# Graph network of eight convolutions on one core: edge rows stay in their PSUM bank through product and scans, TensorE mixes the two Eve scans and adds the residual, swish becomes one activation

## The chip, the cores and the metric

One Trainium2 chip, one of its cores. The metric is the device time of one execution in microseconds (us); lower is better. The kernel before takes 11591.99 us, the median of 3 runs (11556.57 to 11599.9).

## The reference

Node rows `x` (100000 x 128, float32) go through eight graph convolutions, one after the other. There are 50000 edges `src -> dst`, sorted by `dst`. Everything is float32.

```python
# three GCN layers
norm = dinv[src2] * ew2 * dinv[dst2]
out = segment_sum(norm[:, None] * (x @ W)[src2], dst2) + b     # then a residual, batch norm and relu
# two Eve layers
p = relu(x @ wpool.T + bpool); m = p[src]
xmax, xmin = segment_max(m, dst), segment_min(m, dst)           # 0 for a node without edges
eve = relu(wconv[0] * xmax + wconv[1] * xmin + bconv[0])
out = x @ wself.T + eve @ weve.T + bias                         # relu after the first; layer norm of (out + x0) after the second
# two Sage layers
out = segment_mean(x[src], dst) @ W_l.T + b + x @ W_r.T         # h * sigmoid(h) after the first; layer norm of (out + x0) after the second
# one attention layer (GAT) at the end, not touched here
```

## The kernel before, in words

The program runs in stages, with a barrier after each: constants, index tables, degrees (`deg`), the GCN stages `m0`, `m1`, `m2`, a stage `n3` of nodes alone, the Eve stages `m4` (ends with relu) and `m5` (ends with a layer norm, adds the residual stream `x0`), the Sage stages `m6` (ends with swish) and `m7` (ends with a layer norm, adds `x0`), and the attention stage `g8`. The tiles of `m0` to `m7` all have the prefix `m_` in the profile, those of `g8` have `g_`.

A stage `m0` to `m7` does two things at once. **Edges** come in 49 chunks of 1024 (`CH`), a chunk in two halves of 512. GpSimd (POOL) gathers a chunk's rows by 8 indirect DMAs of 128 rows (L1011), and it later scatters the chunk's results into the table `sums` by 8 more (L1019); in between it copies 16 indices for a chunk (L998). In its program the scatters of a chunk come four or five chunks after the gathers. TensorE turns a half with four transposes into a PSUM bank (`e_turn`, `turn_half`, L1060). VectorE (DVE) then reduces over runs of edges with the same `dst` with `tensor_tensor_scan` along the free axis, with a 0/1 mask `same_run`. TensorE multiplies the result with the weights (`multiply_half`, L1070, bank `e_out`), and VectorE writes it to `result`, from where it is scattered. **Nodes** come in 49 pairs of chunks (a unit). SP loads `y`, `x0` where there is one, and `sums` (`load_nodes`, L1095 to L1104) into one buffer for each chunk of a pair, then issues a fill of the next stage's `sums` (L1111). TensorE turns `y` (L1128), ScalarE (ACT) copies it to `nodeT` (L1154, L1156), TensorE multiplies (L1139), VectorE adds `sums`, ScalarE finishes and issues the store.

`merged_sweep` sets the order on every engine but POOL: an edge unit of two chunks (four halves), then the node units whose sums are ready, at most two for an edge unit. Each engine runs its part in program order. SP issues a unit's load of `sums` after it has waited for the scatters that it depends on (L1103).

What the change touches, by stage:

- **GCN edges** (`m0` to `m2`): in `m1` and `m2` ScalarE copies the bank with a scale and a shift to the SBUF tile `hT` (L1293). `weigh` (L1308) multiplies with the weights `w_all` into `hT`, from `hT` in `m1` and `m2`, from the bank in `m0`. The scan (L1329) reads `hT`.
- **GCN nodes**: `res_b = residual + sums`, both in SBUF, 128x1024 elements for one chunk (L1615).
- **Eve edges** (`m4`, `m5`): ScalarE copies the bank to `xT` (L1419), TensorE multiplies by `wpool` (L1375, bank `pool`), ScalarE takes relu to the SBUF tile `pT` (L1433). VectorE scans `hi` (max, L1462) and `lo` (min, L1467) from `pT`, then mixes: `mix = lo * wconv[1] + bconv` (L1474) and `mix = hi * wconv[0] + mix` (L1478). ScalarE takes relu of `mix` (L1407), TensorE multiplies.
- **Norm nodes** (`m5`, `m7`): `part = sums + x0`, both in SBUF, 128x1024 for one chunk (L1717), then `z` = bank + `part` (L1732). The layer norm is applied by ScalarE in sixteen activations for a unit (L743).
- **Swish nodes** (`m6`): ScalarE takes the sigmoid of `z` into `o` (L1774), VectorE multiplies `o * z`, both in SBUF, 128x1024 for one chunk (L1752).

The scan of the Sage stages (L1529) reads its edge rows from the PSUM bank `e_turn` already.

## Time and profile before

| | |
|---|---|
| Median of 3 runs | 11591.99 us (11556.57 to 11599.9) |
| Profiled execution: span from its first to its last instruction | 11581.2 us |
| Median less the span of the profiled execution | 10.8 us |
| PE busy | 6121.9 us (53%) |
| DVE busy | 6779.3 us (59%) |
| ACT busy | 4593.8 us (40%) |
| POOL busy | 7662.4 us (66%) |
| Mean granted TensorE clock | 0.752 of full speed |

The page gives no other time of the profiled execution than its span. Busy shares are means over stages that differ: the seven convolution stages take some 7,750 us of the span, `g8` some 2,250, `n3` some 560. An engine's busy time counts neither its DMA issues (for SP and ACT) nor its waits. On POOL an indirect DMA does count, for the time in which POOL makes its descriptors.

### The profile page before, as it was taken

Reading aid. Unit: us, or ns where it says so; the run is one execution under the profiler, and the core shown is the slowest. Engines: PE = TensorE matmul, PEld = TensorE weight load, DVE = VectorE, ACT = ScalarE, POOL = GpSimd, SP = SyncE. Lnnn points to the kernel's source line nnn. Section 1 sums busy time; section 2 is a strip of 40 time slices with the busy share of each in tenths; the row PEclk is TensorE's granted clock in tenths of the full one; section 3 lists DMA queues with packets and bytes.
Section 4 is the critical chain, followed back from the end, with each engine's and each line's share of the span. In section 5 each row is a group of like instructions: output and inputs, shape, how many; then the busy total and the mean of one; then the engine's idle time right before and its main releaser. Section 6 shows DMA issues by size and latency. Waiting matters only on the chain. (4 is left out here: it accounts for less than half of the span.)

```text
span 11581.2 us, 165045 instructions
## 1 busy us (share of the span) xinstructions
PE 6121.9 (53%) x35574; PEld 4955.3 (43%) x35575; DVE 6779.3 (59%) x16578; ACT 4593.8 (40%) x8654; POOL 7662.4 (66%) x7581
## 2 busy tenths in 40 slices
PE   1005666666566669865655554554454544444443
PEld 1005565566565653354444443544454422222221
DVE  3325555555555556555547775444466647777777
ACT  1111211222222225444435554333355546666665
POOL 4657776777677750177777775777777765666652
PEclk6557887788788889887877777777677766676675
DMA  5997777888788878676657776766688833333322
GB/s 140 223 192 230 260 253 232 283 296 302 250 290 301 297 260 285 224 244 239 226 199 270 259 256 201 256 240 241 216 313 285 291 107 106 110 102 111 110 96 79
DMA packets 1864913, 2570.41 MB, mean 222 GB/s; under 512 B 255773, under 2 KB 1369141, under 8 KB 1864662
## 3 DMA queue, kind: packets, MB, share of 16 engines
q1 hardware_dynamic: 1134168, 1627.27, 42.3%
q10 hardware_dynamic: 504726, 564.87, 14.9%
q0 software_dynamic: 225792, 375.94, 10.1%
q14 instruction: 169, 1.38, 0.0%
q8 instruction: 58, 0.95, 0.0%
HBM read 1499.62 MB, written 1129.98 MB: 227 GB/s over the span
## 5 line engine op out<-in xcount | busy, mean ns | idle before, releaser
L1128 PE MATMUL m_n_bank<-k_ident,m_in_y 128*128 128x128 f32 x5488 | 1009.4, 355 | 1549.2 <-DMA m_in_y<-node_rows_a 396.1
L1019 POOL DMA_INDIRECT sums_gcn<-m_result,m_idx x1176 | 1305.4, 1110 | 420.7 <-issue 348.6
L1128 PEld LDWEIGHTS m_n_bank<-k_ident,m_in_y 128*128 128x128 f32 x5488 | 865.9, 186 | 1648.7 <-issue 1067.6
L1011 POOL DMA_INDIRECT m_rows<-node_rows_a,m_idx x1176 | 1217.6, 1035 | 339.4 <-issue 335.2
L1154 ACT ACTIVATE m_nodeT<-m_n_bank 128x512 f32<-128x512 f32 x980 | 547.3, 597 | 1985.9 <-PE m_n_bank L1128 1973.0
L1019 POOL DMA_INDIRECT sums_eve<-m_result,m_idx x784 | 857.1, 1093 | 348.1 <-issue 231.9
L1019 POOL DMA_INDIRECT sums_sage<-m_result,m_idx x784 | 800.9, 1022 | 263.2 <-issue 230.7
L1011 POOL DMA_INDIRECT m_rows<-node_rows_b,m_idx x784 | 798.2, 1018 | 226.2 <-issue 225.2
L1060 PE MATMUL m_e_turn<-k_ident,m_rows 128*128 128x128 f32 x2744 | 529.5, 328 | 691.1 <-DVE m_sums L1529 327.0
L2181 POOL DMA_INDIRECT sums_gat<-g_result,g_idx x392 | 427.2, 1090 | 669.6 <-DVE g_result L2437 555.8
L1628 DVE SCALAR_TENSOR_TENSOR m_acc<-m_n_bank,m_scales,m_res_b 128x128 f32<-128x128 f32 (+1 forms) x2352 | 634.1, 342 | 264.7 <-PE m_n_bank L1139 204.3
L1060 PEld LDWEIGHTS m_e_turn<-k_ident,m_rows 128*128 128x128 f32 x2744 | 415.3, 173 | 816.4 <-DVE m_sums L1529 319.9
L1573 PE MATMUL m_gram<-m_y 128*128 128x129 f32 (+1 forms) x4800 | 613.1, 288 | 151.2 <-ACT m_y L1599 149.6
L743 ACT ACTIVATE m_o<-m_z,m_ln_shift,m_ln_scale 128x128 f32<-128x128 f32 x1600 | 626.4, 479 | 163.4 <-DMA node_rows_c<-m_o 105.4
L1905 POOL DMA_INDIRECT degree<-deg_deg_slot,deg_place_slot x392 | 452.0, 1153 | 327.4 <-DVE deg_deg_slot L1982 216.9
L1573 PEld LDWEIGHTS m_gram<-m_y 128*128 128x128 f32 (+1 forms) x4800 | 585.1, 201 | 174.8 <-ACT m_y L1599 173.4
L1615 DVE TENSOR_TENSOR m_res_b<-m_in_x,m_in_sums 128x1024 f32<-128x1024 f32 x196 | 240.2, 1226 | 648.0 <-DMA m_in_sums<-sums_gcn 646.5
L1156 ACT ACTIVATE m_nodeT<-m_n_bank,k_bn 128x512 f32<-128x512 f32 x392 | 285.5, 776 | 826.3 <-PE m_n_bank L1128 825.8
L1139 PE MATMUL m_n_bank<-k_gcn,m_nodeT 128*128 128x128 f32 (+1 forms) x4704 | 606.3, 285 | 0.0
L1070 PE MATMUL m_e_out<-k_gcn,m_sums 128*128 128x128 f32 x2352 | 417.3, 333 | 322.8 <-DVE m_result L1341 322.0
L1139 PEld LDWEIGHTS m_n_bank<-k_gcn,m_nodeT 128*128 128x128 f32 (+1 forms) x4704 | 586.8, 203 | 0.0
L998 POOL COPY m_idx<-k_edge_idx 128x16 int32 (+1 forms) x350 | 107.7, 310 | 715.9 <-POOLq L104 715.1
(295 smaller groups left out, 17377.3 us busy)
## 6 DMA issues: line engine op xcount, KB each, us to landing
m_in_sums<-sums_gcn SPq DMA_DIRECT2D x291, 512.0 KB
m_in_y<-node_rows_a SPq DMA_DIRECT2D x291, 512.0 KB
sums_gcn<-k_gcn_b SPq DMA_DIRECT2D x194, 512.0 KB
node_rows_a<-m_y ACTq DMA_DIRECT2D x194, 512.0 KB
...
```

What stands on the lines that cost most here:

```text
L743: ins = act.activation(out[0:n, j, :], z[0:n, j, :], ACT.Identity, bias=self.shift[copy][0:n, at:at + 1], scale=self.scale[copy][0:n, at:a ...
L1011: pool.indirect_dma_start(self.rows[b][:, t, :], None, self.table[:, :], bass.IndirectOffsetOnAxis(self.idx[s][:, t:t + 1], 0)).then_inc(s ...
L1019: pool.indirect_dma_start(self.node_sums[:, :], bass.IndirectOffsetOnAxis(self.idx[s][:, T + t:T + t + 1], 0), self.result[b][:, t, :], No ...
L1060: mm = pe.transpose(bank[:, n * P:(n + 1) * P], self.rows[b][:, H * (i % 2) + n, 0:D], self.k["ident"][:, :])
L1070: mm = pe.matmul(bank[:, n * D:(n + 1) * D], lhs[:, n * P:(n + 1) * P], weight[:, :], start=True, stop=True)
L1128: mm = pe.transpose(self.n_bank[i][:, t * P:t * P + n], self.buf["y"][i // 2][0:n, H * (i % 2) + t, :], self.k["ident"][0:n, 0:n])
L1139: mm = pe.matmul(self.n_bank[i][0:n, t * D:(t + 1) * D], self.nodeT[:, i, t * P:t * P + n], weight[:, :], start=True, stop=True)
L1154: act.activation(out, src, ACT.Copy).then_inc(self.n_turn_read, 1)
L1573: mm = pe.matmul(self.gram[:, 0:D + 1], self.y1[b][0:rows[b], t, 0:D], self.y1[b][0:rows[b], t, :], start=False, stop=False, skip_group_ch ...
L1628: ins = dve.scalar_tensor_tensor(out=self.acc[b][0:n, tt, :], in0=ph.node_out(i, n)[:, t, :], scalar=self.scales[b][0:n, tt:tt + 1], in1=s ...
L1905: pool.indirect_dma_start(self.dram["degree"][:, :], bass.IndirectOffsetOnAxis(self.place_slot[s][:, t:t + 1], 0), self.deg_slot[b][:, t:t ...
L2181: pool.indirect_dma_start(self.node_sums[:, :], bass.IndirectOffsetOnAxis(self.idx[s][:, T + t:T + t + 1], 0), self.result[b][:, t, :], No ...
```

## The change

The copies `hT`, `pT` and `part` in SBUF go. Products and relus write back into the PSUM bank that they read, and the scans read the bank. So a bank is free for the next half only after the scan (GCN: `self.summed`; Eve: the bank holds the pooled rows, then the mix, until `mix_relu`). In Eve, TensorE makes the mix with two 128x512 matmuls with diagonal matrices `mix_w` (made once, among the constants), and ScalarE adds the bias in its relu. The order of TensorE's and ScalarE's steps within an Eve edge unit changes. In the norm stages TensorE adds `x0` in the bank with an identity matmul of 128x512 ahead of each bank's product. `res_b` is made in four pieces of 256 elements. Swish is one `Silu` activation.

```diff
+PIECE = 2
 # constants, VectorE, once
+                for i in (1, 2):
+                    for m in range(2):
+                        dve.tensor_scalar(k[f"mix{i}"][:, m, :], k["ident"][:, :], k[f"wconv{i}"][:, m:m + 1], None, ALU.mult).then_inc(mix_made, 1)
...
 # Conv.multiply_nodes
+            if add:
+                if i % 2 == 0:
+                    self.have(pe, add, m, i // 2)
+                half = self.buf[add][i // 2][0:n, H * (i % 2):H * (i % 2) + H, :]
+                mm = pe.matmul(self.n_bank[i][0:n, :], self.k["ident"][0:n, 0:n], half.rearrange("p t f -> p (t f)"), start=True, stop=False)
+                if i % 2:
+                    mm.then_inc(self.used[add], 1)
             for t in range(H):
                 mm = pe.matmul(self.n_bank[i][0:n, t * D:(t + 1) * D], self.nodeT[:, i, t * P:t * P + n], weight[:, :],
-                               start=True, stop=True)
+                               start=not add, stop=not add or t == H - 1)
...
 # GcnEdges
-                self.ph.turn_half(pe, j, par, q, i, self.turn_free)
+                self.ph.turn_half(pe, j, par, q, i, self.summed)
...
-            act.activation(self.hT[:, i % 2, :], ph.e_turn[i % ph.turn_banks][:, :], ACT.Identity, bias=ss[:, 1:2],
-                           scale=ss[:, 0:1]).then_inc(ph.e_turn_read, 1)
+            act.activation(bank[:, :], bank[:, :], ACT.Identity, bias=ss[:, 1:2], scale=ss[:, 0:1]).then_inc(ph.e_turn_read, 1)
...
-        dve.tensor_tensor(self.hT[:, i % 2, :], src, w, ALU.mult).then_inc(self.weighted, 1)
+        dve.tensor_tensor(bank[:, :], bank[:, :], w, ALU.mult).then_inc(self.weighted, 1)
...
-                                       self.hT[:, i % 2, :], start, ALU.mult, ALU.add).then_inc(self.summed, 1)
+                                       ph.e_turn[i % ph.turn_banks][:, :], start, ALU.mult, ALU.add).then_inc(self.summed, 1)
...
 # EveEdges.tensor
-            wait_from(pe, self.pooled, g - 1)
+            wait_from(pe, self.mix_relu, g - 1)
...
+        def mix(jj, i):
+            g = 4 * jj + i
+            pe.wait_ge(self.hi_done, g + 1)
+            pe.wait_ge(self.lo_done, g + 1)
+            pe.matmul(self.bank[i % 2][:, :], self.mix_w[:, 0, :], self.hi[:, i % 2, :], start=True, stop=False)
+            pe.matmul(self.bank[i % 2][:, :], self.mix_w[:, 1, :], self.lo[:, i % 2, :], start=False, stop=True).then_inc(self.mixed, 1)
...
         for i in range(halves):
+            before_half(mix, i)
+            if i + 1 < halves and i:
+                ph.turn_half(pe, j, par, q, i + 1, ph.e_turn_read)
+            before_half(multiply, i)
             if i == 0:
                 pool(0)
-            if i + 1 < halves:
-                ph.turn_half(pe, j, par, q, i + 1, ph.e_turn_read)
-            multiply_before(i)
+                if halves > 1:
+                    ph.turn_half(pe, j, par, q, 1, ph.e_turn_read)
             if i + 1 < halves:
                 pool(i + 1)
...
 # EveEdges.scalar
-            act.activation(self.mix[:, i, :], self.mix[:, i, :], ACT.Relu).then_inc(self.mix_relu, 1)
+            act.activation(self.mix[:, i, :], self.bank[i % 2][:, :], ACT.Relu, bias=self.bconv[:, 0:1]).then_inc(self.mix_relu, 1)
...
-            act.activation(self.pT[:, i % 2, :], self.pool_ps[i % 2][:, :], ACT.Relu, bias=self.bpool[:, 0:1]).then_inc(self.pooled, 1)
+            act.activation(self.bank[i % 2][:, :], self.bank[i % 2][:, :], ACT.Relu, bias=self.bpool[:, 0:1]).then_inc(self.pooled, 1)
...
         for i in range(halves):
+            if i == 0 and back:
+                relu(j - 1, back - 1)
             copy(i)
             begin(i)
             pool(i)
-            relu_before(i)
+            if i:
+                relu(j, i - 1)
...
 # EveEdges.vector: both scans read the bank, and mix(i) goes
-            dve.tensor_scalar(self.mix[:, i, :], self.lo[:, i % 2, :], self.wconv[:, 1:2], self.bconv[:, 0:1], ALU.mult,
-                              ALU.add).then_inc(self.lo_scaled, 1)
-            dve.scalar_tensor_tensor(out=self.mix[:, i, :], in0=self.hi[:, i % 2, :], scalar=self.wconv[:, 0:1], in1=self.mix[:, i, :],
-                                     op0=ALU.mult, op1=ALU.add).then_inc(self.mixed, 1)
...
 # GcnNodes.vector
-            dve.tensor_tensor(self.res_b[b][0:n, :, :], ph.buf[self.res][b][0:n, :, :], ph.buf["sums"][b][0:n, :, :],
-                              ALU.add).then_inc(ph.used[self.res], 1)
+            for t in range(0, T, PIECE):
+                ins = dve.tensor_tensor(self.res_b[b][0:n, t:t + PIECE, :], ph.buf[self.res][b][0:n, t:t + PIECE, :],
+                                        ph.buf["sums"][b][0:n, t:t + PIECE, :], ALU.add)
+            ins.then_inc(ph.used[self.res], 1)
...
 # LinearNodes
-        self.ph.multiply_nodes(pe, m, self.weight)
+        self.ph.multiply_nodes(pe, m, self.weight, add="x0" if self.finish == "norm" else None)
...
-                dve.tensor_tensor(self.part[b][0:n, :, :], ph.buf["sums"][b][0:n, :, :], ph.buf["x0"][b][0:n, :, :],
-                                  ALU.add).then_inc(ph.used["sums"], 1)
...
-            rest = self.part[b] if norm else ph.buf["sums"][b]
-            dve.tensor_tensor(self.z[b][0:n, half, :], ph.node_out(i, n), rest[0:n, half, :], ALU.add).then_inc(ph.n_out_read, 1)
+            dve.tensor_tensor(self.z[b][0:n, half, :], ph.node_out(i, n), ph.buf["sums"][b][0:n, half, :], ALU.add).then_inc(ph.n_out_read, 1)
             if i % 2:
                 ph.read_node(dve, m, i)
+                dve.sem_inc(ph.used["sums"], 1)
...
-                dve.tensor_tensor(self.o[b][0:n, :, :], self.o[b][0:n, :, :], self.z[b][0:n, :, :], ALU.mult).then_inc(self.ph.finished, 1)
...
-                f, done = (ACT.Relu, ph.finished) if self.finish == "relu" else (ACT.Sigmoid, self.gated)
-                act.activation(self.o[b][0:n, :, :], self.z[b][0:n, :, :], f).then_inc(done, 1)
+                act.activation(self.o[b][0:n, :, :], self.z[b][0:n, :, :], ACT.Relu if self.finish == "relu" else ACT.Silu).then_inc(ph.finished, 1)
```

## Rows read from the trace of the kernel before

**Rows 1.** Stretches m0, m1, m2, m4 to m7: PE, PEld, DVE, ACT, POOL busy, clock, DMA.

```profile
900.00:1990.00 1090.00, 696.35 (x5102) 654.39 (x5102) 620.42 (x1579) 213.27 (x343) 838.43 (x831) 0.83 0.76 250
2012.00:3132.00 1120.00, 718.90 (x5098) 673.83 (x5098) 621.14 (x1576) 313.36 (x392) 867.63 (x831) 0.81 0.84 288
3156.00:4275.00 1119.00, 711.45 (x5098) 667.74 (x5098) 620.15 (x1576) 313.63 (x392) 862.72 (x831) 0.82 0.84 288
...
4865.00:5939.00 1074.00, 640.78 (x3724) 528.14 (x3724) 549.41 (x683) 433.98 (x686) 835.14 (x831) 0.79 0.66 229
5956.00:7154.00 1198.00, 690.85 (x3724) 551.92 (x3724) 872.03 (x1891) 650.46 (x1421) 862.80 (x831) 0.76 0.72 248
7184.00:8222.00 1038.00, 516.97 (x3528) 500.58 (x3528) 465.46 (x806) 333.56 (x392) 798.91 (x831) 0.74 0.69 237
8241.00:9298.00 1057.00, 528.27 (x3528) 507.08 (x3528) 674.21 (x1916) 554.56 (x1127) 807.35 (x831) 0.72 0.80 281
```

**Rows 2.** Timeline of m1: start, duration, engine, line, tiles, idle before and releaser.

```profile
2505.89 0.97 POOL L1019 DMA_INDIRECT sums_gcn<-m_result,m_idx  x1 [0.30 <-issue]
...
2506.86 0.20 POOL L998 COPY m_idx<-k_edge_idx 128x16 int32 x1
...
2513.59 0.95 POOL L1011 DMA_INDIRECT m_rows<-node_rows_a,m_idx  x1 [0.30 <-issue]
2514.28 1.23 DVE L1615 TENSOR_TENSOR m_res_b<-m_in_x,m_in_sums 128x1024 f32<-128x1024 f32 x1 [0.59 <-DMA m_in_sums<-sums_gcn]
2514.84 1.49 POOL L1011 DMA_INDIRECT m_rows<-node_rows_a,m_idx  x1 [0.30 <-issue]
```

**Rows 3.** Timeline of m7, whose scan reads the PSUM bank.

```profile
8701.43 1.27 DVE L1529 TENSOR_TENSOR_SCAN m_sums<-k_same_run,m_sums,m_e_turn 128x512 f32<-128x512 f32 x1
...
8701.49 0.97 POOL L1019 DMA_INDIRECT sums_sage<-m_result,m_idx  x1 [0.30 <-issue]
```

**Rows 4.** Groups of VectorE's instructions by line, stage m1: busy, mean ns | idle before.

```profile
L1329 DVE TENSOR_TENSOR_SCAN m_sums<-k_same_run,m_sums,m_hT 128x512 f32<-128x512 f32 (+1 forms) x97 | 123.6, 1274 | 0.1
L1615 DVE TENSOR_TENSOR m_res_b<-m_in_x,m_in_sums 128x1024 f32<-128x1024 f32 x96 | 117.6, 1226 | 302.1 <-DMA m_in_sums<-sums_gcn 301.5
...
L1308 DVE TENSOR_TENSOR m_hT<-m_hT,m_w_all 128x512 f32<-128x512 f32 x98 | 66.0, 674 | 40.8 <-ACT m_hT L1293 40.4
```

**Rows 5.** Waits of SP's queue, m1: us in total, times, longest.

```profile
SPq L1103 <- DMA sums_gcn<-m_result,m_idx: 334.7, 40, 22.3
```

**Rows 6.** Waits of SP's queue, m4.

```profile
SPq L1103 <- DMA sums_eve<-m_result,m_idx: 512.6, 44, 78.4
```

**Rows 7.** Waits of SP's queue, m7.

```profile
SPq L1103 <- DMA sums_sage<-m_result,m_idx: 375.4, 40, 69.1
```

**Rows 8.** Waits of SP's queue, m5.

```profile
SPq L1095 <- ACTq L1149: 370.0, 37, 18.8
...
SPq L1103 <- DMA sums_eve<-m_result,m_idx: 99.2, 3, 78.2
```

**Rows 9.** Waits of the compute engines, m5: us in total, times, longest.

```profile
POOL sums_eve L1019 <- DVE m_result L1449: 107.4, 16, 25.1
```

**Rows 10.** Timeline of m5, an edge unit.

```profile
6532.52 2.07 PE L1375 MATMUL m_pool<-m_xT,k_pool 128*128 128x512 f32 x2 [8.70 <-ACT m_xT L1419]
...
6536.95 1.02 PE L1375 MATMUL m_pool<-m_xT,k_pool 128*128 128x512 f32 x2
...
6539.96 1.27 DVE L1462 TENSOR_TENSOR_SCAN m_hi<-k_same_run,m_hi,m_pT 128x512 f32<-128x512 f32 x1
...
6540.19 1.13 PE L1070 MATMUL m_e_out<-k_eve,m_mix 128*128 128x128 f32 x8 [1.77 <-ACT m_mix L1407]
...
6542.21 0.69 ACT L1433 ACTIVATE m_pT<-m_pool,k_bpool 128x512 f32<-128x512 f32 x1 [1.11 <-PE m_pool L1375]
...
6544.36 1.27 DVE L1462 TENSOR_TENSOR_SCAN m_hi<-k_same_run,m_hi,m_pT 128x512 f32<-128x512 f32 x1
...
6545.00 1.42 POOL L1019 DMA_INDIRECT sums_eve<-m_result,m_idx  x1 [0.30 <-issue]
```

More of the change, by code:

```diff
@@ L1130, in turn_nodes, with multiply_nodes @@
             mm.then_inc(self.n_turned, 1)
-    def multiply_nodes(self, pe, m, weight, between=None):
+    def multiply_nodes(self, pe, m, weight, between=None, add=None):
         for i in range(4):
@@ L1353, in __init__ @@
         self.wpool, self.weve, self.bpool = k[f"pool{no}"], k[f"eve{no}"], k[f"bpool{no}"]
-        self.wconv, self.bconv, self.bias = k[f"wconv{no}"], k[f"bconv{no}"], k[f"eve_r{no}"]
-        self.xT, self.begin, self.pT, self.hi, self.lo = (ph.sb(n, [P, 2, HALF]) for n in ("xT", "begin", "pT", "hi", "lo"))
+        self.mix_w, self.bconv, self.bias = k[f"mix{no}"], k[f"bconv{no}"], k[f"eve_r{no}"]
+        self.xT, self.begin, self.hi, self.lo = (ph.sb(n, [P, 2, HALF]) for n in ("xT", "begin", "hi", "lo"))
         self.mix = ph.sb("mix", [P, 4, HALF])
-        self.pool_ps = [ph.ps(f"pool{i}", [P, HALF]) for i in range(2)]
+        self.bank = [ph.ps(f"pool{i}", [P, HALF]) for i in range(2)]
         self.pooled_ps, self.pooled, self.begun = ph.sem("pooled_ps"), ph.sem("pooled"), ph.sem("begun")
         self.hi_done, self.lo_done = ph.sem("hi_done"), ph.sem("lo_done")
-        self.lo_scaled, self.mixed, self.mix_relu = ph.sem("lo_scaled"), ph.sem("mixed"), ph.sem("mix_relu")
+        self.mixed, self.mix_relu = ph.sem("mixed"), ph.sem("mix_relu")
     def sync(self, sp, j, par, q, halves, back):
@@ L1399, in tensor @@
         if halves == 0:
-            multiply_before(0)
+            before_half(mix, 0)
+            before_half(multiply, 0)
     def scalar(self, act, j, par, q, halves, back):
@@ L1438, in scalar @@
             pool(i)
-            relu_before(i)
-        if halves == 0:
-            relu_before(0)
+            if i:
+                relu(j, i - 1)
+        if halves == 0 and back:
+            relu(j - 1, back - 1)
     def vector(self, dve, j, par, q, halves, back):
@@ L1681, in __init__ @@
         self.z, self.o = ([ph.sb(f"{n}{b}", [P, T, D]) for b in range(2)] for n in ("z", "o"))
-        if finish == "norm":
-            self.part = [ph.sb(f"part{b}", [P, T, D]) for b in range(2)]
-        self.z_done, self.gated = ph.sem("z_done"), ph.sem("gated")
+        self.z_done = ph.sem("z_done")
         if finish == "norm":
@@ L1710, in vector @@
         self.finish_vector(dve, m)
-        if norm:
-            dve.wait_ge(ph.n_out_read, 4 * m + 4)
-            for b in range(2):
-                n = ph.sh.rows(m * 2 + b)
-                ph.have(dve, "sums", m, b)
-                ph.have(dve, "x0", m, b)
-                dve.tensor_tensor(self.part[b][0:n, :, :], ph.buf["sums"][b][0:n, :, :], ph.buf["x0"][b][0:n, :, :],
-                                  ALU.add).then_inc(ph.used["sums"], 1)
         for i in range(4):
@@ L1737, in vector @@
                 else:
-                    dve.sem_inc(ph.used["sums"], 1)
                     dve.sem_inc(self.z_done, 1)
@@ L1747, in finish_vector @@
             self.ln.solve_scale(dve, m)
-        if self.finish == "swish":
-            for b in range(2):
-                n = self.ph.sh.rows((m - 1) * 2 + b)
-                dve.wait_ge(self.gated, 2 * m + b + 1)
-                dve.tensor_tensor(self.o[b][0:n, :, :], self.o[b][0:n, :, :], self.z[b][0:n, :, :], ALU.mult).then_inc(self.ph.finished, 1)
     def vector_end(self, dve):
@@ L2537, in build @@
         keep("zeros", [P, D + 1], stack=early)
+        for n in ("mix1", "mix2"):
+            keep(n, [P, 2, D], stack=early)
         keep("bn_cols", [P, 2, D], stack=early)
```

55 lines of the change are left out of this document (18 added, 37 removed).

## The prediction, made before the changed kernel was run

> **What bounds the kernel now.** I read first the busy time by stretch [rows 1]. In each of the seven convolution stages POOL has the same work, 831 counted instructions: 392 gathers, 392 scatters and 47 index copies. It is POOL that is busy for the same 75 to 78% of six of the seven stages, while the other engines differ widely (DVE 45 to 64%). The timeline says what the rest is: 0.30 us of issue ahead of each indirect DMA, with no wait for anything [rows 2]. So POOL runs through, one DMA every 1.25 to 1.27 us, and each microsecond that an indirect DMA takes longer is a microsecond of the stage. Only m5 differs: 1198 us long, DVE 73%, and POOL waits there for VectorE's results for 107 us [rows 1, 9].
>
> Next, SP's waits. SP can issue a unit's `sums` only when the scatters are through. In m1 it waits for them 40 times, 335 us in all [rows 5], in m4 for 513 us [rows 6], in m7 for 375 us [rows 7]. That is the slack of everything behind POOL: the edge and node work could run faster than POOL lets it. In m5 this wait is 99 us, 78 of it one wait at a time, and SP waits for the node buffers instead (370 us) [rows 8]. So m0, m1, m2, m4, m6 and m7 go at POOL's pace, m5 at that of its own loop through ScalarE, VectorE and TensorE.
>
> **What lengthens POOL's instructions.** The shortest gather takes 0.95 us and the shortest scatter 0.97, an index copy 0.20 [rows 2]. A stage at these durations has 392 x 0.95 + 392 x 0.97 + 47 x 0.20 = 762 us of POOL busy. Over that lie [rows 1]: m0 76, m1 106, m2 101, m4 73, m5 101, m6 37, m7 45 us. A gather that starts at 2514.84, in the middle of VectorE's L1615 (two SBUF inputs, until 2515.51), takes 1.49 us: 0.54 more, so it is held until 0.13 us ahead of the end of L1615 [rows 2]. A scatter that starts at 6545.00 within the `hi` scan (until 6545.63) takes 1.42, held until 0.18 ahead of the scan's end [rows 10]. In m7 a scatter starts 0.06 us into a scan of the same length and takes 0.97 [rows 3]: that scan reads its rows from PSUM and only the mask from SBUF. So a VectorE instruction holds POOL up when both its inputs are in SBUF, and not when one is in PSUM.
>
> The size checks out. An instruction of length L, met at random by a DMA every 1.27 us and blind in its last b, costs (L - b)^2 / (2 x 1.27). For m1 [rows 4]: scan 1.27, b 0.19: 0.46 x 98 = 45 us; L1615 1.226, b 0.13: 0.473 x 98 = 46; L1308 0.674: 0.117 x 98 = 11. Together 102, against the 106 of the table.
>
> The Trainium skill, page "SBUF — State Buffer", section "Who interferes with whom", has the same rule: VectorE with two SBUF inputs and a GpSimd instruction that reads SBUF exclude one another for the whole instruction, and one with a PSUM input does not. The trace agrees, 0.54 us and nothing. But the same section has a remark that speaks against this change: that `tensor_tensor` did not stall DMAs from GpSimd, because writing descriptors needs the other half of the port. By that remark the change would free nothing; it is rival D.
>
> **The change part by part.**
>
> *GCN.* `hT` goes to the bank: product and scan have one SBUF input each (`w_all`, the mask) and hold POOL no more. L1615 keeps its two SBUF inputs, but in four pieces. From 0.674 us for 512 elements and 1.226 for 1024 [rows 4] a piece of 256 takes some 0.40 (an estimate); four cost 4 x 0.27^2 / 2.54 = 0.115 us against 0.473, so 24% stays. L1615's share is 46 us in m1 and m2, and 76 x 46 / 91 = 38 in m0, where L1308 reads PSUM already and the rule gives 45 + 46 = 91. Gains: m0 76 - 9 = 67, m1 106 - 11 = 95, m2 101 - 11 = 90. The new wait, turn g for the scan of g - 2, holds TensorE while VectorE is busy with half g - 1 for at least 1.9 us (0.67 + 1.27, and the results between them); a turn and ScalarE's copy fit in it, and if not, a microsecond of wait in each half, 98 us a stage, is still inside SP's slack of 335. Behind TensorE's wait stands only the product of the half before, which VectorE asks for later. Three more VectorE instructions for a chunk lie in the idle time before L1615 (302 us in m1 [rows 4]).
>
> What an in-place write to PSUM costs VectorE and ScalarE no row shows. Nearest are L1308 (0.674) and L1433 (0.69). I take them unchanged; at the other end twice as long, 98 x 0.67 = 66 us a stage, inside the slack of 335. A gain is not excluded but would not show either.
>
> *Eve, m4.* The scans read PSUM, L1474 and L1478 go, TensorE gets two more 128x512 matmuls. The 73 us of m4 go. TensorE's added work is at most 2 x 2.07 us a half [rows 10], 406 us in all, against 513 us in which SP waits for POOL. I count it hidden.
>
> *m6 and m7.* The product `o * z` and `part` are the only two-SBUF instructions of length there: 37 and 45 us go. `Silu` instead of sigmoid is one activation for one. In m7 TensorE gets four 128x512 matmuls for a node unit, 49 x 4 x 1.02 = 200 us (406 at 2.07) and is busy for half of the stage; hidden by the 375 us of slack. The release of `sums` moves from `part` to the end of `z`, which is how m6 works already.
>
> *m5.* POOL's pace doesn't set this stage, so its 101 us are not counted. A half of an edge unit takes 4.40 us now (from scan to scan), with VectorE full [rows 10]. Two scans of 1.27 and a result of some 0.67 leave 1.2 us of it for L1474 and L1478. After the change VectorE loses these 1.2 us a half, but TensorE, in order, has: mix 2 x 1.02, wait for relu (0.69 and two hand-overs, 1.0, an estimate), product 1.13, pool 1.02: 5.2 us. That is 0.8 more for three halves; the last half's mix goes to the front of the next unit, where product and relu now precede the first pool (+1.8), VectorE's last mix is gone (-1.2), and TensorE comes to the first pool with work behind it: 1.02 instead of 2.07 (-1.0), its higher level of 2.4 GHz and its lower of 1.2. Sum 3 x 0.8 + 1.8 - 1.2 - 1.0 = +2.0 us, x 24.5 units = +49, less some 14 (a choice) in the first part of the stage where POOL kept pace: +35. The `x0` matmuls (4.1 us a unit) lie beside ScalarE's norm. `part` leaves VectorE while `z` waits for ScalarE anyway: nothing.
>
> *Constants:* four small instructions, under 2 us.
>
> **The sum.** 67 + 95 + 90 + 73 + 37 + 45 = 407 us. The floor of 762 takes the shortest duration of each form, which not every instruction reaches, and waits of POOL for its own DMAs grow a little. I take nine tenths: 366. With +35 for m5: -331. Against the profiled execution: span 11581 - 331 = 11250. The median of the runs lies 11 above that span: 11261 us.
>
> **The rivals.**
>
> A, as above, m5 within 80 us of that: 11261. Chance 0.60.
>
> B, m5 gets shorter too. For it: VectorE is its busiest engine (73%) and loses 98 x 1.2 + 98 x 1.23 (`part`, of L1615's shape) = 238 us, and POOL loses its 101 us there. Against: the scans wait for ScalarE and TensorE as well. At the end it is as long as m4 will be, 1074 - 73 = 1001: -197 instead of +35, total 11029. Chance 0.15.
>
> C, slower: TensorE becomes the bound of m5. For it: in-order work per half grows from 3.2 to 5.2 us at the high clock, and at the low one (2.07 for a 128x512) to 4.1 + 1.0 + 2.2 + 2.07 = 9.4. Then m5 takes 98 x 5.0 = 490 more, total 11592 - 366 + 490 = 11716. It decides from 4.40 + 366 / 98 = 8.1 us a half. Against: TensorE that is busy without a pause ran its later pools at 1.02 [rows 10]. Chance 0.05.
>
> D, the holding-up isn't by SBUF inputs, and nothing is freed: 11592 + 35 = 11627. Against it stand rows 2, 3 and 10. Chance 0.05.
>
> E, POOL is faster but something else takes over in the six stages. m1 moves 288 GB/s x 1120 us = 323 MB; in 1025 us that is 315 GB/s at a DMA share of 0.92 instead of 0.84 [rows 1], so loads land later. With half the gain lost: 11592 - 183 + 35 = 11444. Chance 0.15.
>
> **How the numbers follow.** Likeliest is A. The range reaches towards B and over E: 11130 to 11450. Half a per cent, 58 us, is about what a measurement of this kernel can tell from no change. Faster by more: A, B, E: 0.90, less a little for the end of E, 0.89. Slower: C and half of D. Same: the rest.
>
> **What would show it.** Right, if POOL busy falls to about 770 to 785 in each stage (m1 from 868), gathers stay near 0.95 and scatters near 0.97 on the mean, the only longer ones beside L1615's pieces, and m1 is near 1030, m4 near 1005, m6 near 1003, m7 near 1015 us long; SP still waits for scatters in the hundreds of us. Step m5 is right if it is 1150 to 1280 long with halves of about 5 us. Wrong, if scatters within scans from PSUM with an in-place product still take 1.2 to 1.9 us; if SP's wait for scatters vanishes in m1, m4 or m7; or if m5's matmuls run at 2.07.

## The result, and the profile after

The changed kernel takes 11174.5 us (median of 4 runs, 11172.2 to 11186.6); the kernel before, run beside it, 11594.2. The ratio is 0.9645, 95% interval 0.9632 to 0.9657: 420 us less. The forecast was 11261, within 11130 to 11450; the time is 87 us under it. The profiled execution's span is 11184.0 us, against 11581 before. In three later calls, each on another chip, the kernel before took 15.1 ms, and variants of the changed kernel came out 1.5 to 3.8% slower than it; see the last experiments.

Busy time by stretch of the kernel after, one row for each of m0, m1, m2, m4, m5, m6 and m7, as in [rows 1]:

```profile
core 0: us, PE busy (x) PEld busy (x) DVE busy (x) ACT busy (x) POOL busy (x), PEclk, DMA share, GB/s
889.00:1919.00 1030.00, 699.69 (x5102) 650.26 (x5102) 639.58 (x1867) 213.47 (x343) 779.08 (x831) 0.86 0.81 264
1944.00:2982.00 1038.00, 718.48 (x5098) 669.66 (x5098) 641.35 (x1864) 311.32 (x392) 778.31 (x831) 0.86 0.93 311
3007.00:4046.00 1039.00, 699.21 (x5098) 647.80 (x5098) 640.92 (x1864) 310.70 (x392) 778.56 (x831) 0.88 0.91 311
4638.00:5647.00 1009.00, 768.86 (x4116) 541.80 (x4116) 427.69 (x487) 436.47 (x686) 765.35 (x831) 0.90 0.74 244
5664.00:6827.00 1163.00, 930.14 (x4508) 602.75 (x4508) 638.13 (x1599) 652.31 (x1421) 765.56 (x831) 0.94 0.74 255
6855.00:7863.00 1008.00, 497.30 (x3528) 478.44 (x3528) 351.07 (x708) 333.70 (x392) 765.65 (x831) 0.74 0.71 244
7880.00:8895.00 1015.00, 704.23 (x3920) 567.01 (x3920) 561.54 (x1820) 553.11 (x1127) 765.80 (x831) 0.80 0.84 292
```

POOL's busy time was 799 to 868 us a stage; it is 778 to 779 in the GCN stages and 765 or 766 in the other four. The stages became shorter by 60, 82, 80, 65, 35, 30 and 42 us: 394 of the 397 us between the two spans. POOL's work is unchanged (831 instructions). So the six stages in which POOL set the pace gave 359 of the 394 us. VectorE fell from 872 to 638 us in m5, TensorE rose from 691 to 930, at a granted clock of 0.94 instead of 0.76.

An edge unit in m5, timeline of after, to be read against [rows 10]. All four `hi` scans (L1477) of the unit stand in it:

```profile
6502.57 1.28 DVE L1477 TENSOR_TENSOR_SCAN m_hi<-k_same_run,m_hi,m_pool 128x512 f32<-128x512 f32 x1 [3.11 <-ACT m_pool L1445]
...
6505.52 1.27 DVE L1477 TENSOR_TENSOR_SCAN m_hi<-k_same_run,m_hi,m_pool 128x512 f32<-128x512 f32 x1
...
6507.98 1.16 PE L1078 MATMUL m_e_out<-k_eve,m_mix 128*128 128x128 f32 x8 [0.42 <-ACT m_mix L1426]
...
6509.27 0.69 DVE L1464 TENSOR_TENSOR m_result<-m_e_out,k_eve_r 128x512 f32<-128x512 f32 x1 [1.31 <-PE m_e_out L1078]
...
6509.84 1.02 PE L1388 MATMUL m_pool<-m_hi,k_mix 128*128 128x512 f32 x2
...
6510.69 1.02 PE L1389 MATMUL m_pool<-m_lo,k_mix 128*128 128x512 f32 x2
...
6510.82 1.28 DVE L1477 TENSOR_TENSOR_SCAN m_hi<-k_same_run,m_hi,m_pool 128x512 f32<-128x512 f32 x1 [0.86 <-ACT m_pool L1445]
...
6511.52 0.97 POOL L1027 DMA_INDIRECT sums_eve<-m_result,m_idx  x1 [0.30 <-issue]
...
6511.83 0.69 ACT L1426 ACTIVATE m_mix<-m_pool,k_bconv 128x512 f32<-128x512 f32 x1 [1.13 <-PE m_pool L1389]
6512.02 1.26 DVE L1481 TENSOR_TENSOR_SCAN m_lo<-m_begin,m_lo,m_pool 128x512 f32<-128x512 f32 x1
...
6512.57 1.16 PE L1078 MATMUL m_e_out<-k_eve,m_mix 128*128 128x128 f32 x8 [0.42 <-ACT m_mix L1426]
...
6515.41 1.28 DVE L1477 TENSOR_TENSOR_SCAN m_hi<-k_same_run,m_hi,m_pool 128x512 f32<-128x512 f32 x1 [0.95 <-ACT m_pool L1445]
```

The scatter of 6511.52 starts within the `hi` scan of 6510.82, which now reads PSUM, and takes 0.97 us; the one shown in [rows 10] within the same scan from SBUF took 1.42. From one `hi` scan to the next it is now 2.95, 5.30 and 4.59 us within the unit, where each of the three took 4.41 to 4.43 before (medians over the stage; for after they are the values of this unit). The two mixes take 1.02 us each, the product waits 0.42 us for the relu behind them.

VectorE's groups in m1 by shape (last columns: busy us, mean ns, idle ahead and its releasers), then SP's wait for scatters in m1, in m4 and in m7:

```profile
L1618 DVE TENSOR_TENSOR m_res_b<-m_in_x,m_in_sums 128x256 f32<-128x256 f32 x384 | 137.7, 420 | 64.1 <-DMA m_in_sums<-sums_gcn 63.3
...
L1315 DVE TENSOR_TENSOR m_e_turn<-m_e_turn,m_w_all 128x512 f32<-128x512 f32 x98 | 66.9, 683 | 38.6 <-ACT m_e_turn L1306 38.1
```

```profile
SPq L1111 <- DMA sums_gcn<-m_result,m_idx: 208.3, 36, 19.4
```

```profile
SPq L1111 <- DMA sums_eve<-m_result,m_idx: 271.0, 33, 70.3
```

```profile
SPq L1111 <- DMA sums_sage<-m_result,m_idx: 319.5, 36, 68.9
```

A piece of 256 elements takes 0.420 us (0.40 was the estimate), the product written back into PSUM 0.683 (0.674 to SBUF before, [rows 4]): the in-place write costs 9 ns. SP (its wait is now L1111) still waits 208, 271 and 320 us for scatters, where it was 335, 513 and 375 [rows 5, 6, 7]. POOL still sets the pace there: in m1 its busy time and 784 issues of 0.30 us make 1013 of the 1038 us.

### The profile page after: what moved, and what is told of

Its sections match the earlier page's. It is cut to its first block and busy times, and to the rows that moved or that the text cites. A ratio compares the mean times of both kernels' runs of the same rounds, so it can differ in the third digit from the quotient of the medians.

```text
span 11184.0 us, 167613 instructions
## 1 busy us (share of the span) xinstructions
PE 6640.9 (59%) x37142; PEld 5031.2 (45%) x37143; DVE 6252.3 (56%) x16776; ACT 4592.8 (41%) x8654; POOL 7206.7 (64%) x7581
## 5 line engine op out<-in xcount | busy, mean ns | idle before, releaser
L1027 POOL DMA_INDIRECT sums_gcn<-m_result,m_idx x1176 | 1163.5, 989 | 432.3 <-issue 350.6
L1136 PE MATMUL m_n_bank<-k_ident,m_in_y 128*128 128x128 f32 x5488 | 851.9, 313 | 914.2 <-DMA m_in_y<-node_rows_c 383.3
L1019 POOL DMA_INDIRECT m_rows<-node_rows_a,m_idx x1176 | 1130.0, 961 | 339.3 <-issue 331.5
L1721 DVE TENSOR_TENSOR m_z<-m_n_bank,m_in_sums 128x512 f32<-128x512 f32 (+1 forms) x784 | 506.1, 686 | 1320.5 <-ACT m_o L1757 372.7
L1136 PEld LDWEIGHTS m_n_bank<-k_ident,m_in_y 128*128 128x128 f32 x5488 | 721.7, 162 | 1006.2 <-issue 816.9
L1027 POOL DMA_INDIRECT sums_eve<-m_result,m_idx x784 | 762.6, 973 | 415.5 <-issue 230.0
L1019 POOL DMA_INDIRECT m_rows<-node_rows_b,m_idx x784 | 755.5, 964 | 226.1 <-issue 223.4
L1575 PE MATMUL m_gram<-m_y 128*128 128x129 f32 (+1 forms) x4800 | 681.9, 306 | 315.9 <-ACT m_y L1601 314.3
L1575 PEld LDWEIGHTS m_gram<-m_y 128*128 128x128 f32 (+1 forms) x4800 | 645.5, 218 | 349.0 <-ACT m_y L1601 347.7
L1078 PE MATMUL m_e_out<-k_gcn,m_sums 128*128 128x128 f32 x2352 | 388.0, 316 | 297.1 <-DVE m_result L1348 296.8
L2156 POOL DMA_INDIRECT g_src_rows<-node_rows_b,g_idx x392 | 444.7, 1135 | 112.7 <-issue 112.7
```

The costliest lines, as they stand in the source:

```text
L1019: pool.indirect_dma_start(self.rows[b][:, t, :], None, self.table[:, :], bass.IndirectOffsetOnAxis(self.idx[s][:, t:t + 1], 0)).then_inc(s ...
L1027: pool.indirect_dma_start(self.node_sums[:, :], bass.IndirectOffsetOnAxis(self.idx[s][:, T + t:T + t + 1], 0), self.result[b][:, t, :], No ...
L1136: mm = pe.transpose(self.n_bank[i][:, t * P:t * P + n], self.buf["y"][i // 2][0:n, H * (i % 2) + t, :], self.k["ident"][0:n, 0:n])
L1575: mm = pe.matmul(self.gram[:, 0:D + 1], self.y1[b][0:rows[b], t, 0:D], self.y1[b][0:rows[b], t, :], start=False, stop=False, skip_group_ch ...
L1721: dve.tensor_tensor(self.z[b][0:n, half, :], ph.node_out(i, n), ph.buf["sums"][b][0:n, half, :], ALU.add).then_inc(ph.n_out_read, 1)
L2156: pool.indirect_dma_start(rows[b][:, t, :], None, self.table[:, :], bass.IndirectOffsetOnAxis(self.idx[s][:, at:at + 1], 0)).then_inc(self ...
```

## The experiments

Times in the first four runs stand beside 11593.4 us for the kernel before (7 runs on that chip), and beside 11174.5 for after, which was measured in an earlier call. Fences with a diff are shortened. The scatters of the degree stage, which no edit touches, span 778 us in the trace of before, 765 in that of after and 786, 790, 793 and 789 in those of e1 to e4: up to 28 us of a difference in total against after say nothing of an edit, so the readings go by stage.

**e1_gcn_bank_only.** The kernel before with one part of the change: the GCN edges keep ScalarE's copy and the product in the bank, the scan reads it there, the sum of residual and `sums` stays one instruction.

```diff
-        turn_half(..., self.turn_free)   # product -> hT in SBUF
+        turn_half(..., self.summed)      # product in place in the bank
```

> The kernel before with the GCN edge part of the change alone: the half stays in its bank through ScalarE's copy, product and scan; L1615 is whole, Eve, Sage and node parts are as before. Theory (VectorE instructions with both inputs in SBUF hold POOL up, and m0 to m2 go at POOL's pace): m0 -35, m1 -60, m2 -55 us, other stages unchanged, 11594 - 150 = 11444. POOL busy in m1 falls from 868 to about 810, the whole L1615 keeps the rest. Rival 1 (the gain comes from VectorE and ScalarE having less to do): they run the same instructions here, so no gain, 11594. Rival 2 (the longer wait of the turn for the scan costs something): less than half of 150.

11437.9 us, ratio 0.987 (0.9854 to 0.9887): 156 less. Busy time of m1:

```profile
1989.00:3049.00 1060.00, 720.13 (x5098) 667.32 (x5098) 619.46 (x1576) 312.08 (x392) 806.39 (x831) 0.86 0.89 305
```

m1 went from 1120 to 1060 us, m0 and m2 by 35 and 58. The scan and the product alone give 153 us over the three stages, with VectorE's work unchanged. A rival by which `tensor_tensor` and the scan don't hold POOL up falls here.

**e2_one_piece.** After, with the sum in one piece.

```diff
-PIECE = 2
+PIECE = 8
```

> The changed kernel with PIECE = 8, so that res_b of a chunk is one instruction of 128x1024 again. Theory (each instruction holds POOL for itself, and POOL gets in between two): by (L - b)^2 / (2 x 1.27) one of 1.226 us costs 0.473 and four of 0.40 cost 0.115, 98 times in each of three stages: at most +105 us; as the same rule gave too much for m0, I expect +80, 11254, with POOL busy near 805 in m0 to m2. Rival (pieces issued back to back hold POOL like one long instruction, and the change gained all in the scans): within 20 us of 11174.

11275.4 us (0.973, 0.9714 to 0.9746): 101 more than after. m1, busy time:

```profile
1993.00:3053.00 1060.00, 722.63 (x5098) 669.50 (x5098) 619.82 (x1576) 311.91 (x392) 803.95 (x831) 0.86 0.90 304
```

POOL is 26 us busier in m1 than in after, and the stage 22 longer; m0, m1 and m2 together are 75 longer. The two profiled spans differ by 84 us: these 75, the 25 of the degree scatters, and 16 less in what no edit touches. Cutting a two-input instruction in four is worth about 25 us a stage.

**e3_x0_on_vector.** After, with `part = sums + x0` back on VectorE in m5 and m7.

```diff
-        multiply_nodes(pe, m, self.weight, add="x0" ...)
+        multiply_nodes(pe, m, self.weight)
...
+                dve.tensor_tensor(self.part[b][0:n, :, :], ph.buf["sums"]..., ph.buf["x0"]..., ALU.add)
```

> The changed kernel with the residual of m5 and m7 back on VectorE (part = sums + x0, 128x1024, both in SBUF), TensorE without the x0 matmuls. m7: +40 us by the theory (POOL is held by part). m5, which got 35 us shorter where I had forecast 35 longer: theory A (TensorE's added matmuls raised its granted clock from 0.76 to 0.94 and so shortened the serial chain of a node unit) gives m5 +40 to +80 with a clock of 0.85 or less; theory B (VectorE's relief by the Eve mix, or POOL's release, shortened m5) leaves m5 within 15 us of 1163. In all 11215 by B, 11260 to 11295 by A.

**e4_eve_as_before.** After, with the whole of `EveEdges` as before in m4 and m5: scans from SBUF, mix by L1474 and L1478, relu from SBUF.

> The changed kernel with the Eve edges of before (pT in SBUF, mix on VectorE, no mix matmuls), x0 still added by TensorE. m4: +60 us by the theory (hi, lo and mix hold POOL again). m5: my forecast had the new edge order as a cost of some 50 us a stage; if so m5 gets 20 to 60 us shorter than 1163 here. If the new edge order is a gain in m5 (theory A through the clock, theory B through VectorE's relief), m5 gets longer, to 1180 or more. In all 11174 + 60 - 40 = 11194 by my forecast, over 11250 if both stages gained.

e3 took 11286.7 us (0.9733, 0.9716 to 0.9749), e4 11243.1 (0.9701, 0.9685 to 0.9717): 112 and 69 more than after. Busy time of m5 and m7 in e3, then of m4 and m5 in e4:

```profile
5682.00:6902.00 1220.00, 837.21 (x4116) 592.02 (x4116) 752.99 (x1695) 651.54 (x1421) 798.22 (x831) 0.83 0.71 243
7956.00:9013.00 1057.00, 536.27 (x3528) 513.09 (x3528) 673.80 (x1916) 554.05 (x1127) 804.43 (x831) 0.72 0.81 281
```

```profile
4650.00:5722.00 1072.00, 642.09 (x3724) 531.15 (x3724) 549.45 (x683) 434.96 (x686) 834.43 (x831) 0.80 0.67 230
5739.00:6887.00 1148.00, 805.04 (x4116) 576.19 (x4116) 758.00 (x1795) 649.59 (x1421) 826.33 (x831) 0.86 0.75 258
```

m7 goes back to the 1057 us of before and m4 to 1072, of 1074. In m5 the four kernels make a square:

| m5, us (clock) | Eve edges before | Eve edges new |
|---|---|---|
| x0 on VectorE | 1198 (0.76), before | 1220 (0.83), e3 |
| x0 on TensorE | 1148 (0.86), e4 | 1163 (0.94), after |

The edge part costs m5 15 to 22 us; moving x0 saves 50 to 57. The forecast had +35 for the first and nothing for the second. The two corners from the earlier calls hold on the chip of e3 and e4 too: m5 takes 1198 us in e1, which has before's code there, and 1167 in e2, which has after's. In e4 the two stages pull in opposite directions (+63 and -15); the other 21 us of its 69 are about the difference in the degree scatters.

Where in a unit do they fall? From the last `hi` scan of a unit to the first of the next, a stretch that holds the node work, the median is 34.2 us in before, 31.8 in e4, 35.8 in e3 and 33.3 in after: moving x0 takes 2.4 to 2.6 us from it, the new edge part adds 1.5 to 1.6. The three intervals within the unit together take, in the same order, 13.3, 13.3, 13.1 and 12.8 us.

What does the 50 consist of? ScalarE's wait ahead of the norm's activations in m5 (before, e3, e4, after in this order):

```profile
L743 ACT ACTIVATE m_o<-m_z,m_ln_shift,m_ln_scale 128x128 f32<-128x128 f32 x784 | 306.9, 479 | 121.6 <-DMA node_rows_c<-m_o 105.4 <-DVE m_ln_shift L732 16.2
```

```profile
L751 ACT ACTIVATE m_o<-m_z,m_ln_shift,m_ln_scale 128x128 f32<-128x128 f32 x784 | 306.9, 479 | 112.0 <-DMA node_rows_c<-m_o 96.6 <-DVE m_ln_shift L740 15.4
```

```profile
L751 ACT ACTIVATE m_o<-m_z,m_ln_shift,m_ln_scale 128x128 f32<-128x128 f32 x784 | 307.8, 480 | 72.8 <-DMA node_rows_c<-m_o 56.6 <-DVE m_ln_shift L740 16.1
```

```profile
L751 ACT ACTIVATE m_o<-m_z,m_ln_shift,m_ln_scale 128x128 f32<-128x128 f32 x784 | 307.8, 479 | 63.2 <-DMA node_rows_c<-m_o 47.6 <-DVE m_ln_shift L740 15.5
```

With x0 on VectorE it waits 105 and 97 us for its own stores of `m_o`, with x0 on TensorE 57 and 48. VectorE in turn waits for these activations, and POOL for VectorE; the largest such waits in m5 of after:

```profile
DVE m_z L1721 <- ACT m_o L751: 179.4, 50, 5.2
POOL sums_eve L1027 <- DVE m_result L1464: 171.5, 22, 26.4
```

The saving of 49 us in this wait, for either edge part, is nearly that of the stage (50 and 57); that the one makes the other is argued from this, not shown. Three things could be behind it: TensorE's clock, VectorE's load, or the order in which x0 and `sums` are released and loaded, which changes when the stores get the DMA engines. The square speaks against the clock alone: both parts raise it, the new edge part by 0.07 and 0.08, x0's move by 0.10 and 0.11, and yet m5 gets longer by the one and shorter by the other. Four kernels were meant to tell them apart and to measure two more points; they ran on other chips.

**e5_swish_as_before, e6_one_input, e8_unused_matmuls, e9_unused_part.** In one call; the kernel before took 15121.2 us on that chip.

```diff
 e5: after, m6
-   act.activation(o, z, ACT.Silu)
+   act.activation(o, z, ACT.Sigmoid); dve.tensor_tensor(o, o, z, ALU.mult)
 e6: after, m6
+   dve.tensor_scalar(spare, z, 2.0, None, ALU.mult)
 e8: e3, m5 and m7, ahead of each node product; result unused
+   pe.matmul(self.n_bank[i][:, :], ident, self.nodeT[:, i, :], start=True, stop=True)
 e9: after, m5 and m7, where part stood; result unused
+   dve.tensor_tensor(self.part[b], sums, sums, ALU.add)
```

> The kernel after with swish in m6 as it was before: ScalarE's sigmoid and VectorE's 128x1024 product of two SBUF inputs. Theory: the product alone makes m6 some 30 us longer, as POOL is held up again (busy 766 to about 797 us): 11174 + 30 = 11204 us (11195 to 11215). Rival: m6 became shorter because one activation does the work and the stores start earlier, not through POOL; then POOL's busy time stays at 766 us and the stage is longer all the same.

> The kernel after with one more VectorE instruction for each node chunk in m6: a 128x1024 tensor_scalar from SBUF to SBUF, with one input only, 98 times; its result isn't read. Theory A: only an instruction with two SBUF inputs holds up POOL. Then POOL's busy time in m6 stays at 766 us and the time at 11174 (11165 to 11185). Theory B: any instruction of VectorE between SBUF and SBUF does. At a length of some 1.1 us it adds 0.37 us for each, 36 us in all: POOL's busy time in m6 is about 800 us and the time about 11210.

> The kernel after with x0 back on VectorE in m5 and m7, as in the run e3_x0_on_vector (11286.7 us; m5 1220 us long at a granted clock of 0.83, m7 1056), and with the four 128x512 matmuls of a node unit kept on TensorE, whose result nobody reads. Theory A: the 50 to 57 us that x0 on TensorE gives m5 come from TensorE's clock, which its added work raises. Then m5 falls back to about 1165 us at a clock of about 0.93, m7 stays at 1056, and the time is about 11232 us (11220 to 11245). Theory B: they come from VectorE, which loses the 1.23 us additions ahead of the node results. Then m5 stays at 1215 us or more, whatever the clock, and the time is 11280 to 11340.

> The kernel after (11174 us), x0 still added by TensorE, with one more 128x1024 addition of two SBUF inputs on VectorE for each chunk in m5 and m7, where the addition of x0 stood before; its result isn't read. Theory A (clock): m5 stays near 1165 us, since TensorE's work and clock are unchanged, m7 rises by the 41 us for which POOL is held up: about 11215 (11205 to 11230). Theory B (VectorE): m5 rises to about 1220, m7 to about 1056, and the time is about 11272 (11255 to 11290).

e5 15706.3 us (1.0368, 1.0336 to 1.04), e6 15650.8 (1.0348, 1.0314 to 1.0383), e8 15673.1 (1.0359, 1.0317 to 1.0402), e9 15656.6 (1.0348, 1.0317 to 1.038). None of the expected times can be read off: all of them are 3.5 to 3.7% above the kernel before on this chip. What can be read is inside the stages. m6 of e5, then m5 and m6 of e6:

```profile
10060.00:11574.00 1514.00, 599.45 (x3528) 547.21 (x3528) 467.30 (x806) 336.45 (x392) 781.58 (x831) 0.64 0.51 163
```

```profile
8135.00:9995.00 1860.00, 1028.41 (x4508) 678.74 (x4508) 638.49 (x1599) 653.60 (x1421) 768.07 (x831) 0.77 0.48 159
10023.00:11505.00 1482.00, 538.99 (x3528) 493.20 (x3528) 414.71 (x804) 336.04 (x392) 769.63 (x831) 0.66 0.51 166
```

*POOL, m6.* With the two-input product (1.222 us, 98 times) POOL is busy for 782 us, in e9, which has no extra work there, for 766: +16. That is half of the 31 expected; POOL is idle for much of this longer stage, so fewer of its DMAs can meet the product. m6 is also 32 us longer than in e6, twice what POOL lost. So e5 doesn't rule out its rival, that the one activation itself shortens the stage; for m6 on the first chip there is only that POOL's busy time fell by 33 us and the stage by 30.

With the one-input instruction POOL is at 770, 4 us more than in e9. That small number hides a real hold, timeline of e6:

```profile
10617.52 0.76 DVE L1730 TENSOR_SCALAR m_spare<-m_z 128x1024 f32<-128x1024 f32 x1 [0.15 <-DVE m_z L1722]
10617.88 1.24 POOL L1019 DMA_INDIRECT m_rows<-node_rows_c,m_idx  x1 [0.16 <-issue]
```

The `tensor_scalar` runs at 0.69 us for 1024 elements. A gather that starts 0.36 us into it takes 1.24 instead of 0.95: it is held until 0.11 ahead of the instruction's end. Eight of 9 gathers of over 1.015 us in m6 of e6 lie on such an instruction; e9 has one over 1.015 in all. So theory B of e6 is right in kind: one SBUF input is enough, in this form; the total stays small as the instruction is short and few gathers meet it. The Trainium skill, page "SBUF — State Buffer", section "Who interferes with whom", has this too: `tensor_scalar` in its faster mode takes the pair of ports that GpSimd uses. The trace agrees. The prediction's rule of two SBUF inputs was too narrow.

But not every `tensor_scalar` does it. L1474, which the change removed, has one SBUF input too and takes 0.55 us for 512 elements, where the fast one takes 0.69 for 1024. A gather that begins at its start, timeline of before, m4:

```profile
5478.97 0.55 DVE L1474 TENSOR_SCALAR m_mix<-m_lo,k_wconv,k_bconv 128x512 f32<-128x512 f32 x1
5479.01 1.01 POOL L1011 DMA_INDIRECT m_rows<-node_rows_b,m_idx  x1 [0.16 <-issue]
```

In m4 and m5 of before eight gathers and scatters begin in L1474, each with 0.46 to 0.51 us of it left, and all take 0.97 to 1.01. Held until 0.11 ahead of its end they would have taken 1.3. So its removal freed hardly anything.

*x0, m5.* e8 and e9 were run again (**e8_again**, **e9_again**), on a third chip, where the kernel before was no faster (15136.1 us).

> The kernel of e8_unused_matmuls again, on a chip whose transfers run at the pace of the traces of before and after (if this one does). Theory A, TensorE's clock: m5 about 1165 us at a granted clock of about 0.93, the time about 112 - 55 = 57 us above after, 11232 us. Theory B, VectorE: m5 at 1215 us or more, the time 11280 to 11340.

> The kernel of e9_unused_part again, for the same reason. Theory A, TensorE's clock: m5 near 1165 us and m7 near 1056, the time about 11215 us. Theory B, VectorE: m5 about 1220 us, m7 about 1056, the time about 11272 us.

15723.6 us (1.0377, 1.034 to 1.0415) and 15676.1 (1.0345, 1.0299 to 1.0392). m5 of e8_again, and of e9_again:

```profile
8172.00:10070.00 1898.00, 1052.02 (x4508) 688.26 (x4508) 753.76 (x1695) 653.54 (x1421) 765.29 (x831) 0.76 0.47 156
```

```profile
8143.00:10022.00 1879.00, 1031.09 (x4508) 681.18 (x4508) 749.77 (x1695) 653.80 (x1421) 764.76 (x831) 0.76 0.47 158
```

On these chips m5 takes 1860 and 1866 us in e6 and e5, 1868 and 1879 with VectorE's extra work (e9, twice), and 1911 and 1898 where x0 is really added by VectorE though TensorE does all its matmuls (e8, twice), at nearly the same clock (0.75 to 0.77). So there TensorE's work doesn't explain the difference (it would have put e8 at 1865), and VectorE's not all of it: from e9 to e8 in the same call there are 43 us left on the one chip and 19 on the other. They come with x0's own dependence: who reads it, when it is released, when the next loads start. How much of the 38 to 51 us that is, two pairs that differ by 24 can't say. ScalarE's wait for its stores goes the same way: 77 and 79 us in m5 of e8, 36 and 53 in e9. That this also holds on a chip like the first isn't shown.

**e10_before_again, e11_eve_m5_piece1.** The last call, a fourth chip (before 15111.9 us). e10 is the kernel before, for its trace. e11 is after with two edits in different stages:

```diff
-    run_conv(nc, ph, EveEdges(ph, no), ...)
+    run_conv(nc, ph, (EveEdgesBefore if finish == "norm" else EveEdges)(ph, no), ...)   # m5 only
...
-PIECE = 2
+PIECE = 1
```

> The kernel before, unchanged, for its trace on the chip of this call. If the transfers are as slow as in the last two calls, where this kernel took 15121 and 15136 us and every variant of the changed one 1.035 of it, then the stages of the two traces say where the change costs time there. Theory A: POOL is no bound on such a chip (in e6_one_input it waits 480 to 660 us a stage for VectorE's results), so that freeing it gives nothing, and TensorE's longer hold in the GCN stages (a turn waits for the scan of the half before the last) delays what follows: m0, m1 and m2 are shorter in the kernel before, by most of the 530 us in all, and m6 and m7 are alike. Theory B: the loss lies in all seven stages alike.

> The kernel after with two edits in different stages. In m5 alone the Eve edge part is that of before (x0 stays on TensorE): e4_eve_as_before had m5 at 1147 us with it, against 1163, so 15 us less. In m0, m1 and m2 the sum of x0 and sums is done in eight pieces of 128 elements for each chunk instead of four of 256: of the 14 us over the floor that POOL has left in each, three quarters go, 30 us in all. Theory A, both hold, on a chip with transfers as fast as in the first traces: 11174 - 45 = 11129 us, 0.960 of before. Theory B: VectorE, with some 400 more instructions a stage, becomes the bound of m1; then m0 to m2 get longer and the time is 11160 or more. On a chip with slow transfers: no gain over the 1.035 of the other variants.

e10 took 15152.3 us in its one run, e11 15327.9 (ratio 1.0149, 1.0114 to 1.0183). Busy time of m1, m4 and m5, of e10, then of e11:

```profile
2544.00:4165.00 1621.00, 800.84 (x5098) 716.43 (x5098) 616.87 (x1576) 313.13 (x392) 797.54 (x831) 0.71 0.62 199
6412.00:7895.00 1483.00, 678.46 (x3724) 547.36 (x3724) 552.74 (x683) 428.96 (x686) 813.48 (x831) 0.71 0.52 166
7914.00:9496.00 1582.00, 728.75 (x3724) 572.87 (x3724) 872.33 (x1891) 653.33 (x1421) 833.40 (x831) 0.69 0.58 187
```

```profile
2555.00:4187.00 1632.00, 848.29 (x5098) 762.69 (x5098) 664.85 (x2248) 312.31 (x392) 786.28 (x831) 0.70 0.61 198
6435.00:8061.00 1626.00, 828.48 (x4116) 608.50 (x4116) 429.40 (x487) 432.40 (x686) 764.90 (x831) 0.76 0.46 151
8079.00:9726.00 1647.00, 835.42 (x4116) 599.71 (x4116) 760.88 (x1795) 655.24 (x1421) 814.49 (x831) 0.75 0.55 180
```

Against e10, the stages of e6 (all but m6 have after's code; its chip ran the kernel before in 15121 us) are +21, +41, +19, +153, +278, -27 and +21 us: 506 us, of which m4 and m5 are 431. Both theories of e10 fall: the loss there is neither in the GCN stages nor spread; it lies in the Eve stages. e11 shows that it is their new edge part, by undoing it in m5: 1647 instead of 1860 us, and the ratio falls from 1.035 to 1.015, against what I expected of such a chip. m4, where e11 keeps the new one, stays at 1626. With `PIECE` 1, m0, m1 and m2 take 1620, 1632 and 1631 us against 1630, 1662 and 1650 in e6, but POOL is not less busy (786 against 775 in m1), so the reason given for it fails; whether it helps on a chip like the first was not measured, nor was `after` itself run on one of the others. By e4's 15 us in m5, e11 should beat after on a chip like the first; that stays untried.

What is different on those chips shows in the timeline of e11, end of an edge unit in m4:

```profile
7204.80 2.07 PE L1078 MATMUL m_e_out<-k_eve,m_mix 128*128 128x128 f32 x8 [5.72 <-ACT m_mix L1426]
...
7206.66 3.57 PE L1136 MATMUL m_n_bank<-k_ident,m_in_y 128*128 128x128 f32 x16
...
7220.88 0.69 DVE L1464 TENSOR_TENSOR m_result<-m_e_out,k_eve_r 128x512 f32<-128x512 f32 x1 [17.84 <-issue]
...
7232.06 0.60 ACT L1169 ACTIVATE m_nodeT<-m_n_bank 128x512 f32<-128x512 f32 x1 [27.32 <-remote]
```

TensorE's product L1078 ends at 7206.87. VectorE's `result`, which waits for it, starts at 7220.88, 14.0 us later; in after it takes 0.13 us (6509.14 to 6509.27 above). The four groups of node turns end at 7207.74, 7208.60, 7209.45 and 7210.23; ScalarE, which waits for the first, starts at 7232.06. The semaphore that the turns count up tells the same: its increments are in the trace at 7232.04, 7234.18, 7234.24 and 7234.30, where in after each stands 0.01 us behind its matmul. The instructions take as long as ever. So do the transfers, nearly: the packets of queue q1 took 42.3% of the span before and 33.8% of it in e10, 4900 and 5120 us of the 16 engines. It is the signals, or the ends of the matmuls, that come late; the profile models the end of a matmul, so it can't tell the two apart. The kernel before has it as well: in m4 of e10 ScalarE waits 527 us for such turns, put down to "remote". The traces of these chips also hold fewer than half of the semaphores' increments (99,541 in e10, 211,215 in before, the same kernel), so the waits read in them are rough, and that the slowness comes with the tracing isn't excluded. The new edge part has more signals in a row (scan to TensorE, mix to ScalarE, relu to TensorE), and that fits a loss in m4 and m5; why they are late was not found, nor whether it goes with the chip or with the time of the call.

## Why the prediction was right, and where it was not

**What bounds the six stages.** Right. POOL's busy time fell by 377 us in them, 0.93 of the 407 forecast, and the stages with it: GCN 222 us (forecast 252), m4 65 (73), m6 30 (37), m7 42 (45). The sum is 359; the forecast was 407, and 366 after the cut to nine tenths. e1 and e2 split the GCN part: scan and product gave 153 us (forecast 252 - 99 = 153), the sum in pieces 75 (forecast 29 + 35 + 35 = 99, from [rows 4] with 24% left). POOL has some 14 us over the 765 of the other stages left there, where 9 to 11 were forecast. e4 shows m4 (63), e3 m7 (42); m6 has no run of its own on such a chip.

**Mechanism.** Right for the scans, the products and the sum. The traces show it on far more than the rows that the prediction read. The table has the gathers and scatters that began in an instruction of VectorE with over 0.3 us of it left, and how much longer than the shortest of their kind (0.947, 0.966) they took, as a median:

| instruction | inputs | DMAs | held, us |
|---|---|---|---|
| scan L1329, m1 of before | SBUF, SBUF | 88 | 0.75 |
| sum L1615, m1 of before | SBUF, SBUF | 64 | 0.52 |
| scan L1529, m7 of before | SBUF, PSUM | 76 | 0.005 |
| scan L1336, m1 of after | SBUF, PSUM | 80 | 0.005 |
| product L1315, m1 of after | PSUM in place, SBUF | 27 | 0.005 |
| scans L1477 and L1481, m4 of after | SBUF, PSUM | 156 | 0.005 |
| piece L1618, m1 of after | SBUF, SBUF | 21 | 0.20 |

The rule was too narrow: a one-input `tensor_scalar` in its fast form holds POOL as well (e6). Rival D (nothing is freed) is out by e1, e2 and this table, and with it the remark that the prediction cited for it.

**In-place writes to PSUM.** Counted as unchanged, measured +9 ns.

**m5, +35 us: the step that failed.** The stage came out 35 us shorter. Two terms of its sum were wrong. The first is the edge unit, put at +2.0 us: +2.4 for three halves of 5.2 us instead of 4.4, and -0.4 from the last half to the next unit. Measured from e4 to after, where only the edge part differs, it is -0.4 for the three (2.95, 5.30 and 4.59 against 4.43, 4.41 and 4.41) and +1.5 from the last scan to the next unit's first. So the halves were over-rated and the turn of the unit under-rated; that the sum, +1.1, is still over half of +2.0 is luck, since the two errors partly cancel. The stage pays 15 to 22 us, not 35. In the half of 4.59 the two mixes start 0.85 us apart (6509.84, 6510.69) where 1.02 each was added up, and of the 1.0 us for relu and hand-overs TensorE waits 0.42, since the next turn runs in the rest. The second term, "`part` leaves VectorE while `z` waits for ScalarE anyway: nothing", failed outright: 50 to 57 us. ScalarE, for which `z` waited, itself waited for its stores, and that wait fell by 49 us with x0's move; what in the move does it, x0's order of release and load or VectorE's load, stays open. Rival B had the sign and not the size (-197): m5 still has its own loop.

**The total.** Against the forecast span (11250) the measured one is 66 us less, 70 of it m5. The median lies 10 us under the profiled span instead of 11 above it, the other 21 us. The nine tenths, a choice, came out at 0.88 (359 of 407).

**Rivals C and E.** TensorE ran its mixes at 1.02, not 2.07, and the granted clock of m5 rose from 0.76 to 0.94. DMA share in m1 rose to 0.93 and 311 GB/s, near the 0.92 and 315 computed for E, and cost nothing that shows. On the other chips the sign is that of a slower kernel, by a mechanism that no rival named.
